# Attention slot: mixed values, norms and two short product runs are moved one slot later, into one run

## The reference, cut to what matters

```python
def _L1_attn_ref(x, Wq, Wk, Wv, Wz, Wa, Wb, conv_q_w, conv_k_w, conv_v_w, norm_w, Wout):
    ...
    q = _silu(x @ Wq)
    k = _silu(x @ Wk)
    v = _silu(x @ Wv)
    z = x @ Wz
    ...
    q = _causal_dwconv(q, conv_q_w)
    k = _causal_dwconv(k, conv_k_w)
    v = _causal_dwconv(v, conv_v_w)
    ...
    q = q * cos + rot_half(q) * sin
    k = k * cos + rot_half(k) * sin
    q = q / jnp.maximum(jnp.linalg.norm(q, axis=-1, keepdims=True), 1e-12)
    k = k / jnp.maximum(jnp.linalg.norm(k, axis=-1, keepdims=True), 1e-12)
    ...
    for s in range(K):
        ...
        attn = jnp.einsum('bshd,bshd->bsh', q, k_s) * scale
        gate = jax.nn.sigmoid(a_s * b)
        out = out + (attn * gate)[..., None] * v_s
    ...
    rms = jax.lax.rsqrt(jnp.mean(out * out, axis=-1, keepdims=True) + EPS_NORM)
    out = out * rms * norm_w * _silu(z)
    return out @ Wout
```

## Time and profile before

| | us |
|---|---|
| median of 3 runs | 2850.36 |
| lowest, highest | 2849.88, 2850.41 |
| the profiled execution | 2849.61 |
| its span, first to last instruction | 2847.8 |

### The profile page before, as it was taken

How to read it: one execution, slowest core, us unless ns; L and a number is a source line. 1 busy time by engine, 2 the same in 40 slices (tenths; PEclk the granted TensorE clock), 3 DMA queues, 4 the chain that set the end, 5 groups by cost and what they waited for, 6 DMA issues and landing times. The chain is left out here.

```text
span 2847.8 us, 40066 instructions
## 1 busy us (share of the span) xinstructions
PE 2826.6 (99%) x13466; PEld 2348.4 (82%) x13466; DVE 2252.7 (79%) x3265; ACT 1528.7 (54%) x3149; POOL 1443.2 (51%) x1016
## 2 busy tenths in 40 slices
PE   9999999999999999999999999999999999999998
PEld 7888888888788888888888888778778887888887
DVE  7899587777888889888988898977667677666665
ACT  6656333333666666666666666765545445444443
POOL 7787233334344444444444444666545556555554
PEclk9999999999999999999999999999999999999999
DMA  3000000000322222222222221321111111211111
GB/s 138 1 23 25 12 19 27 30 27 23 125 65 68 70 64 64 65 73 64 64 64 72 77 71 53 93 75 52 52 45 52 60 45 56 86 45 60 52 52 45
DMA packets 79099, 160.44 MB, mean 56 GB/s; under 512 B 11313, under 2 KB 19889, under 8 KB 77873
## 3 DMA queue, kind: packets, MB, share of 16 engines
q1 hardware_dynamic: 78896, 157.88, 18.5%
HBM read 115.63 MB, written 8.65 MB: 44 GB/s over the span
## 5 line engine op out<-in xcount | busy, mean ns | idle before, releaser
L1546 DVE SCALAR_TENSOR_TENSOR x_tok<-OP,expert_weight,x_tok 128x512 f32<-128x512 f32 x252 | 188.1, 748 | 138.2 <-PE OP L47 138.1
L1425 POOL TENSOR_TENSOR middle_w_lo<-second_raw,middle_w_hi 128x512 fp32r<-128x512 f32 (+1 forms) x96 | 143.4, 1496 | 208.7 <-ACT middle_w_hi L1420 208.7
L1518 POOL TENSOR_TENSOR middle_in_lo<-middle_slot,middle_in_hi 128x512 fp32r<-128x512 f32 x128 | 168.6, 1318 | 131.7 <-ACT middle_in_hi L1514 130.9
L3017 POOL TENSOR_TENSOR lag_rnorm<-lag_norm,minus_half 128x8 f32<-128x8 f32 x64 | 105.1, 1643 | 209.5 <-DVE lag_norm L3408 209.5
L45 PE MATMUL B<-xT_hi,lag_w_hi 128*128 128x512 f32 x516 | 201.4, 390 | 1.8 <-DVE xT_lo L496 1.5
L47 PE MATMUL B<-xT_hi,lag_w_lo 128*128 128x512 f32 x516 | 201.6, 391 | 0.0
L45 PE MATMUL A<-xT_hi,lag_w_hi 128*128 128x512 f32 x512 | 200.6, 392 | 0.4 <-DVE xT_lo L496 0.4
L46 PE MATMUL B<-xT_lo,lag_w_hi 128*128 128x512 f32 x516 | 200.8, 389 | 0.0
L47 PE MATMUL A<-xT_hi,lag_w_lo 128*128 128x512 f32 x512 | 199.9, 390 | 0.0
L46 PE MATMUL A<-xT_lo,lag_w_hi 128*128 128x512 f32 x512 | 199.4, 389 | 0.0
L45 PE MATMUL OP<-middle_down_hi,middle_in_hi 128*128 128x512 f32 x496 | 193.6, 390 | 1.9 <-POOL middle_down_lo L1445 1.7
(11 more groups left out here) (670 smaller groups left out, 9103.8 us busy)
## 6 DMA issues: line engine op xcount, KB each, us to landing
lag_raw<-in_head_weights SPq DMA_DIRECT2D x64, 256.0 KB, 4.5
lag_b_row<-lag_b_scratch SPq DMA_DIRECT2D x64, 256.0 KB, 3.3
lag_rot_q<-lag_r SPq DMA_DIRECT2D x128, 128.0 KB, 2.3
lag_rot_k<-lag_r SPq DMA_DIRECT2D x128, 128.0 KB, 2.4
middle_down_raw<-in_expert_down SPq DMA_DIRECT2D x32, 512.0 KB, 3.4
middle_raw<-in_expert_in SPq DMA_DIRECT2D x32, 384.0 KB, 3.0
second_raw<-in_expert_in SPq DMA_DIRECT2D x32, 384.0 KB, 3.0
double_raw<-in_dense_in SPq DMA_DIRECT2D x12, 512.0 KB, 3.4
```

The source lines that it names most:

```text
L1425: pool.tensor_tensor(self.w_lo[q % 2][:, out], self.raw[q % 2][:, of], f32(self.w_hi[q % 2][:, out]), ALU.subtract).then_inc(self.s_wlo, 1)
L1518: pool.tensor_tensor(self.inner_lo[q % 3][t], self.slot((1, 3)[t], q), f32(self.inner_hi[q % 3][t]), ALU.subtract).then_inc(self.s_lo, 1)
L1546: dve.scalar_tensor_tensor(row, self.down_bank(v, n), self.expert_weight[:, e:e + 1], row, op0=ALU.mult, op1=ALU.add).then_inc(self.s_acc, 1)
L3017: pool.tensor_tensor(rnorm[f.rbuf], norm2, half[:, 0:2 * TPB], ALU.pow).then_inc(s_rn, 1)
```

## The change

For slots 2 (`ENTRY`) to 61 (`SWITCH`) each engine has a `lagged_slot` of its own. TensorE's short products stand in one run behind the q/k projections: squares of l1, values of l1, mixed of l3, mix of l2, scores of l1. So squares, mix and mixed come a slot later than before. The turned mix goes to OP1 in place of T. The output projection's tiles 2 and 3 of l3 stand between the v and z projections, and tiles 0 and 1 of l2 behind z. VectorE reduces the squares of l1 (not f) between the taps of `c1` and `c2`, rotates l1 at the start of the slot, and adds tiles of l3 (0 and 1 at the start, 2 and 3 around `y_lo`). GpSimd takes the root of l1 between its two cos products, and its weight splits wait for `s_gain`. Slot 61 catches up with the remaining short products and norms. The last two slots are as before, but that one `accumulate` stands two places later in slot 62, and two weight splits of the expert layer stand behind `c1` there. Nothing is added or taken away: the same products, activations and transfers are issued.

```diff
+        ENTRY, SWITCH = 2, END - 2
+        lagged = lambda f: ENTRY <= f.s <= SWITCH
+        held = lambda f: (2, 3) if f.s == ENTRY + 1 else (0, 1)
...
                 def turn_values(st):
                     pe.wait_ge(s_cv, st.s * TAPS + TAPS)
-                    until(pe, s_osq, st.s - 1 if st.s < SWITCH else st.s)
+                    if st.s > SWITCH - 1:
+                        pe.wait_ge(s_osq, st.s)
+                    else:
+                        until(pe, s_val, st.s)
                     turn_tiles(T, cv, s_vt)
...
+                def lagged_slot(f, l1, l2, l3):
+                    if f.s > ENTRY:
+                        pe.wait_ge(s_pair, l1.s + 1)
+                        pe.wait_ge(s_prob, l1.s)
+                        turn_tiles(S1, squares[0], s_nrm)
+                    turn_values(l1)
+                    if l3:
+                        pe.wait_ge(s_mix, l3.s + 1)
+                        pe.wait_ge(s_acc, l3.s * TPB + held(f)[1] + 1)
+                        turn_tiles(OP1, mixed, s_ot)
+                    if f.s > ENTRY:
+                        mix(l2)
+                    score(l1)
+                    if f.s == ENTRY:
+                        pe.wait_ge(factors.s_c, BATCH)
+                        out_projection(l2, (0, 1))
+                    pe.wait_ge(s_c1, f.s * TAPS + TAPS)
+                    projection(f, 2, A, s_v)
+                    if l3:
+                        pe.wait_ge(s_osq, l3.s + 1)
+                        if f.s > ENTRY + 1:
+                            out_projection(l3, (2, 3))
+                    z_projection(l1, f)
+                    if l3:
+                        out_projection(l2, (0, 1))
+                    else:
+                        out_projection(l2, (2, 3))
+                    if f.s == SWITCH:
...
+                        turn_tiles(T, mixed, s_ot)
+                        mix(l1)
...
+                        turn_tiles(S1, squares[0], s_nrm)
+                        out_projection(l2, (2, 3))
...
+                        turn_tiles(T, mixed, s_ot)
...
+                def lagged_slot(f, l1, l2, l3):
+                    if l3:
+                        sum_squares(l3, OP1)
+                    act.wait_ge(s_c1, f.s * TAPS + TAPS)
+                    act.wait_ge(s_nrm, f.s)
+                    act.activation(squares[0], c1, ACT.Square).then_inc(s_sqr, 1)
+                    if f.s > ENTRY:
+                        mixture(l2)
+                    normed_values(l1)
+                    act.wait_ge(s_v, f.s + 1)
+                    act.activation(A, A, ACT.Silu).then_inc(s_silu, 1)
+                    if f.s > ENTRY:
+                        y_high(l2)
+                    act.wait_ge(s_vt, f.s)
+                    act.wait_ge(s_silu, f.s * 3 + 3)
+                    act.activation(cv, A, ACT.Copy, scale=weight(f, 2, TAPS)).then_inc(s_tap, 1)
+                    act.wait_ge(s_c2, f.s * TAPS + TAPS)
+                    act.activation(squares[1], c2, ACT.Square).then_inc(s_sqr, 1)
+                    gate_z(l1)
...
+                    if lagged(f) and f.s > ENTRY:
+                        root(l1)
                     pool.wait_ge(s_c2, f.s * TAPS + TAPS)
...
+                def lagged_slot(f, l1, l2, l3):
+                    if f.s > ENTRY:
+                        rotated(l1)
+                    gains(l1)
+                    if l3:
+                        for t in held(f):
+                            accumulate(l3, t)
+                    dve.wait_ge(s_tap, f.s * 3 + 1)
+                    tap(0, f, A, c1, 1, s_c1)
+                    tap(0, f, A, c1, 2, s_c1)
+                    tap(0, f, A, c1, 3, s_c1)
+                    if f.s > ENTRY:
+                        sum_of_squares(l1, S1)
+                    dve.wait_ge(s_tap, f.s * 3 + 2)
+                    tap(1, f, B, c2, 1, s_c2)
+                    if f.s > ENTRY:
+                        bounded(l1)
+                    tap(1, f, B, c2, 2, s_c2)
...
+                    tap(1, f, B, c2, 3, s_c2)
+                    if f.s > ENTRY:
+                        gated_output(l2)
+                    probabilities(l1)
+                    if f.s > ENTRY + 1:
+                        accumulate(l3, 2)
...
+                        y_low(l2)
+                    dve.wait_ge(s_tap, f.s * 3 + 3)
+                    tap(2, f, A, cv, 1, s_cv)
+                    if f.s > ENTRY + 1:
+                        accumulate(l3, 3)
+                    tap(2, f, A, cv, 2, s_cv)
+                    tap(2, f, A, cv, 3, s_cv)
```

More of the change, by code:

```diff
@@ L2300, in _ @@
                         factors.product_row(pe, 3)
+                    if lagged(f):
+                        lagged_slot(f, l1, l2, l3)
+                        continue
                     if l1:
@@ L2494, in sum_squares @@
                         tok = st.b * TPB + t
-                        last = act.activation(T[:, t * P:(t + 1) * P], T[:, t * P:(t + 1) * P], ACT.Square,
-                                              scale=at(rnorm[st.rbuf], 2 * t), accum_out=at(ssum, st.head + tok * HEADS))
+                        part = turned[:, t * P:(t + 1) * P]
+                        last = act.activation(part, part, ACT.Square, scale=at(rnorm[st.rbuf], 2 * t), accum_out=at(ssum, st.head + tok * HEADS))
                     last.then_inc(s_osq, 1)
@@ L3015, in _ @@
                     pool.tensor_tensor(squares[0], squares[0], squares[1], ALU.add).then_inc(s_pair, 1)
-                    pool.wait_ge(s_n2, f.s + 1)
-                    pool.tensor_tensor(rnorm[f.rbuf], norm2, half[:, 0:2 * TPB], ALU.pow).then_inc(s_rn, 1)
+                    if not lagged(f) or f.s == SWITCH:
+                        root(f)
                 mean_root(1)
@@ L3327, in _ @@
                 for f, l1, l2, l3 in slots():
-                    inside = l1 and f.s < SWITCH
+                    if lagged(f):
+                        lagged_slot(f, l1, l2, l3)
+                        continue
+                    inside = f.s == ENTRY - 1
                     if l3 and f.s < END:
@@ L3345, in _ @@
                     else:
-                        if l2:
+                        if l2 and f.s == END:
                             accumulate(l2, 0)
@@ L3363, in _ @@
                     tap(1, f, B, c2, 3, s_c2)
-                    if inside and l2:
-                        accumulate(l2, 0)
                     if l2:
+                        if f.s < END:
+                            accumulate(l2, 0)
                         accumulate(l2, 1)
```

115 lines of the change are left out of this document (72 added, 43 removed).

## The result

| | before | after |
|---|---|---|
| median, us | 2850.31 (22 runs) | 2854.16 (22 runs) |
| lowest, highest | 2849.01, 2850.97 | 2853.34, 2854.62 |
| span of the profiled execution | 2847.8 | 2852.7 |

The changed kernel is slower by 3.85 us: ratio 1.0014, 95% interval 1.0008 to 1.002. The forecast was 2848.3, the range ended at 2854.0. The sign was wrong, and the time lies just outside the range. The difference is smaller than the 0.2% (5.7 us) that the prediction took as the least that counts, though the interval leaves out no change.

What follows compares the result with a forecast made beforehand. The prediction took TensorE's product issue to bound the kernel: 2849.61 less 2.4 for merged runs plus 0.35 at the entry gave 2847.6, and a median of 2848.3 us. The 8-in-10 range was 2845.5 to 2854.

Steps and rivals of the forecast that it cites:

- What bounds the kernel: Lag attention: only what TensorE issues, and how closely, sets the time; a regular slot takes 16.80 us.
- One run in place of two: Slots 3 to 61: merging short runs saves 0.04 us a slot, 2.4 us in all, bounds 0.6 and 3.5.
- The score behind the reduction: Regular slots: VectorE's reduction of the squares ends in time for TensorE's score, covered by 0.2 us; cost 0.
- The last tap of cv: Regular slots: VectorE's last tap frees bank A for the next slot, covered by only 0.07 us; cost 0.
- Rival A: Regular slots: the last `cv` tap comes late; 0.1 us late gives 2854, 0.2 late 2860; chance 0.17.
- The first two lagged slots: Slots 2 and 3: fewer products cover the taps, slot 3 frees its bank late; 0.35 us once (0 to 0.6).
- Slot 61 and the end: Catch-up work and extra norms stand beside 20 us of products; value 0, bounds -0.5 and +1 us.
- New waits elsewhere: Turn of `mixed`, sums of squares, GpSimd's weight splits and SyncE's moves in the slots: all covered, value 0.
- B: Regular slots: overhead follows the number of short products, not runs, so nothing is gained; 2850.7 us, chance 0.09.
- C: Regular slots: the whole run overhead goes, 4.7 us, with no entry loss; 2845.7 us, chance 0.08.
- D: Merged run: TensorE's clock falls to 1.2 GHz because of the short products and transposes; 2980 us, chance 0.02.

Runs made afterwards that it cites:

- b_on: Kernel before, with the odd heads' output weights moved 64 bytes onto a 2048-byte border of the partition; 2848.25 us.
- a_fix: a_on without GpSimd's waits for `s_gain`, and in slot 63 VectorE's second and third taps of `cv` ahead of `cross1`; 2851.34 us.
- a_best: a_on with slot 63's taps of `cv` ahead of `cross1`, `s_gain` waits kept, and 65 more already satisfied waits in GpSimd's stream; 2848.04 us.
- a_on: Changed kernel, with the odd heads' output weights moved 64 bytes onto a 2048-byte border of the partition; 2849.51 us.
- b_pad: b_on plus the changed kernel's 45 waits for `s_gain` in GpSimd's stream; 2848.83 us.
- a_32: Changed kernel, with the odd heads' output weights 32 bytes behind a 2048-byte border in place of 64; 2853.26 us.
- a_512: Changed kernel, with the odd heads' output weights 512 bytes ahead of a 2048-byte border; 2849.54 us.

## Why the prediction was wrong, point by point

**What bounds the kernel.** Right: TensorE alone sets the regular slots, and its list of waits stayed empty.

**One run in place of two.** The mechanism was right, the term mis-sized: 0.027 a slot and not 0.04, 1.5 us and not 2.4, inside its bounds of 0.6 to 3.5. The error is worth a second look, since the earlier trace rows held a sign of the answer. I had three values, 0.04, 0.06 and 0.02, took their spread for that of one thing and averaged. The rows of 0.04 and 0.06 are runs ahead of an odd head's output projection, the 0.02 that of an even head, and I even wrote so ("a slot whose head has the other weight buffer"). In b_on, with the place mended, both heads' runs cost the same, 1.367 and 1.800 us. Their products take 0.109 (transposes) and 0.113, so both runs cost 0.03 over them, and the merged run of 3.140 costs 0.02.

**The step that failed** is one the prediction did not have: it moved twelve long products of each slot away from behind the short runs and priced them at 0.2266 wherever they stand. For odd heads each entry from long products costs 0.08, in the shadow of a short run 0.034 on average. That is the +2.70 over 57 slots, and it turned a gain of 1.39 into a loss of 1.31. It is the largest part of the error and not the whole of it: the forecast was 2.05 below the profiled execution before, the medians moved up by 3.85. Of these 5.9 the place made about 2.7, the run that gave less 1.0, the last slots and what follows them some 1.5, the end of the program 0.7 and the entry 0.1.

**The score behind the reduction.** Right that it costs nothing, with less to spare than I said. The reduction ends 0.29 ahead of the load (forecast 0.28), but I took 0.06 for the release, from the earlier trace rows, and a_fix shows 0.22 at this place. So the cover was 0.07 and not 0.2, and in a_fix 0.14 us later costs 0.06 a slot.

**The last tap of cv.** Right that it costs nothing, and VectorE was earlier than I said: it took tile 2 0.43 behind its last product's start (985.19 less 984.76), where the one instance of the earlier trace rows had 0.60. The tap ends 0.24 ahead of the load, where my figures had 0.13 before the release of 0.06. In slot 3, where the load does wait, it comes 0.11 behind the tap, so some 0.13 were to spare, against 0.07. Rival A, which I gave 0.17, did not happen. The time that I had computed for it, 2854, is the time that came, by another way.

**The first two lagged slots.** Right: +0.45 for 0.35, nearly all of it in slot 3 and for the cause named. The wait itself is the 0.30 forecast; the late products behind it, 0.12, were not in the sum.

**Slot 61 and the end.** Wrong: 0 forecast, bounds -0.5 and +1, measured +1.23 and +0.25 behind it. I had counted TensorE's 20 us of products as cover, and for slot 61 that held: up to the turn in slot 62 nothing is lost. Of the 1.23, 0.68 arise up to the turn in slot 63, where TensorE waits for GpSimd's squares, and 0.59 in slot 63. The first part stays in a_best, and no run tests its cause. The second is two instructions that changed places: in b_on VectorE's `cross1` starts first, at 1827.21, takes 0.69, and GpSimd's addition takes 1.75; in the changed kernel GpSimd is 0.10 us ahead, and VectorE's takes 1.74. It is not the luck of one profile: GpSimd is ahead in all six profiles of the changed kernel with its order in slot 63, VectorE in all six with the order before. These rows of b_on stand beside those of the kernel after, above:

```profile
1827.21 0.69 DVE L3381 TENSOR_TENSOR lag_cross<-lag_c,lag_sin 128x512 f32<-128x512 f32 x1
...
1827.31 1.75 POOL L3015 TENSOR_TENSOR lag_square<-lag_square 128x512 f32<-128x512 f32 x1
```

Whoever starts first goes at full speed and the other is held. The Trainium skill ("SBUF — State Buffer", SBUF: two separate sides) calls the port that the two share an exclusive lock which the first to start holds for its whole instruction; the two traces agree, with 1.74 against 0.69 on one side and 1.75 against 1.30 on the other. In a_best, where the two no longer meet, slot 63 is 0.74 shorter than in a_on (14.57 against 15.30).

**New waits elsewhere.** GpSimd's waits held up no other engine, as forecast, and a_fix showed what they are for. They still cost 0.76 us at the end of the program, by b_pad's profile against b_on's: as instructions, not as waits. The Trainium skill ("Runtime: NRT & Kernel Launch", Instruction fetch mechanics) says that the cost of crossing a block of instructions is mostly hidden. Over most of the program these traces agree: the profile after has some 200 fetches, and TensorE's list of waits over the regular slots is empty. At the end of the program a fetch goes with 0.68 to 0.78 us more.

**Rivals B, C and D.** B (nothing gained) has the even heads' 0.027 against it. C did not come, though b_on shows that the odd heads held 1.87 us more that could go. D: the granted clock stayed at 0.999 over the span, the transposes in a run of 3.14 us changed nothing. The 1.2 GHz of the program's start was read from the pace alone, 0.427 us a product against 0.227; the clock column of that row prints 1.00.

## What to carry to other kernels

If rows of one kind differ by more than their rounding, look at the names of their operands before you average them: two classes that alternate can hide a cost of their own, and here a change of order more than doubled it. When long products are moved, price them at the new neighbour, not at their mean pitch. A cover is what is left after the release, so take the release from a row in which the same instruction waits. And at the end of a phase ask whether TensorE still bounds it, and count instructions as well as waits.

## What the runs showed of the hardware

- A moving operand of 128x512 float32 that begins 32 or 64 bytes behind a multiple of 2048 bytes of its partition makes TensorE lose about 0.07 and 0.08 us for six such products within a stream of long ones, spread over some 17 products, those with aligned operands included. 512 bytes off cost nothing (a_32, the changed kernel, a_512).
- Directly behind a short run the same six products cost 0.02 (behind 12 short ones) or 0.047 (behind 16), by the kernel before against b_on.
- A run of 28 short products costs 0.02 over its products at 0.109 (transposes) and 0.113, runs of 12 and 16 cost 0.03, one of four transposes 0.04.
- From the end of VectorE's reduction to the score's weight load that waits for it 0.22 us pass (a_fix), from the last tap to A's 0.11 (slot 3 after).
- Profiles with an 8 KB instruction fetch beside the program's last store take 0.68 to 0.78 us more behind the last product than those without; 45 more instructions in GpSimd's stream brought it there (b_pad), and 65 more than those moved it away (a_best).
